# Order of the recurrent matrix products in one LSTM step: two products of the low part of h moved one place forward

## The reference, cut to what matters

```python
def step(carry, xs):
    h, c = carry
    i_t = sigmoid(xi_t + h @ V_i)
    g_t = tanh(xg_t + h @ V_c)
    o_t = sigmoid(xo_t + h @ V_o)
    c_new = h * c + i_t * g_t
    h_new = o_t * tanh(c_new)
    return (h_new, c_new), h_new
```

## Time and profile before

| what | us |
|---|---|
| median of three runs | 19581.66 |
| lowest, highest | 19550.09, 19586.31 |
| span of the profiled execution | 17545.4 |
| recurrent products in it, from the first to the last | 9353.7 |

### The profile page before, as it was taken

The page is one execution under the profiler, slowest core; times in us unless marked ns, Lnnn a source line. Parts: engine busy times, 40 slices in busy tenths (PEclk is TensorE's granted clock), DMA queues, the critical chain, the costliest instruction groups (busy, mean ns, idle before and its releaser), DMA issues. The chain is left out here.

```text
span 17545.4 us, 683245 instructions
## 1 busy us (share of the span) xinstructions
PE 12730.7 (73%) x250869; PEld 10213.3 (58%) x250870; DVE 11697.3 (67%) x68713; ACT 5986.8 (34%) x41949; POOL 5631.1 (32%) x6174
## 2 busy tenths in 40 slices
PE   5247773399655656556888888888888888888887
PEld 3135552266444544445777777777777777777776
DVE  7368887322555454556777777777777777777777
ACT  0004442011100101003555555554555555555555
POOL 4778887666576575772000000000000000000000
PEclk6558886599877777775555555555555555555555
DMA  0102222111333333331000000000000000000000
GB/s 22 25 21 73 74 72 43 56 34 33 101 105 98 96 105 87 105 105 37 4 4 4 4 4 4 4 4 4 4 4 4 4 4 4 4 4 4 4 4 18
DMA packets 352412, 609.44 MB, mean 35 GB/s; under 512 B 157501, under 2 KB 232222, under 8 KB 348988
## 3 DMA queue, kind: packets, MB, share of 16 engines
q0 software_dynamic: 223104, 471.33, 10.4%
q1 hardware_dynamic: 126524, 100.27, 1.9%
HBM read 508.72 MB, written 62.45 MB: 33 GB/s over the span
## 5 line engine op out<-in xcount | busy, mean ns | idle before, releaser
L2402 PE MATMUL lr_ZI<-ls_h,ls_V 128*128 128x1 f16 x150000 | 5006.8, 166 | 1669.7 <-DVE ls_h L2451 1412.8
L2402 PEld LDWEIGHTS lr_ZI<-ls_h,ls_V 128*128 128x128 f16 x150000 | 4487.3, 104 | 2677.0 <-DVE ls_h L2451 2640.4
L2419 ACT ACTIVATE ls_tg<-lr_ZI 128x2 f32<-128x2 f32 x12500 | 2150.0, 172 | 4626.5 <-PE lr_ZI L2402 4534.6
L2446 DVE TENSOR_TENSOR_SCAN lr_c<-ls_tg,ls_one_hc 128x2 f32<-128x2 f32 x12500 | 2118.1, 170 | 1441.0 <-ACT ls_tg L2419 1317.8
L2358 POOL COPY ls_HT<-ls_h 128x250 f32 x50 | 19.8, 395 | 9358.3 <-DVE ls_h L2456 9358.3
L2402 PE MATMUL lr_ZO<-ls_h,ls_V 128*128 128x1 f16 x75000 | 2865.0, 165 | 0.0
L671 PE MATMUL prop_sum<-prop_G,prop_S 128*128 128x256 f32 x4992 | 1830.4, 546 | 1369.9 <-DMA prop_G<-hop_table,prop_idx 1369.9
L657 POOL DMA_INDIRECT prop_G<-hop_table,prop_idx x2496 | 2368.3, 949 | 1057.3 <-issue 708.8
L2402 PEld LDWEIGHTS lr_ZO<-ls_h,ls_V 128*128 128x128 f16 x75000 | 2483.2, 104 | 0.0
L671 PEld LDWEIGHTS prop_sum<-prop_G,prop_S 128*128 128x128 f32 x4992 | 1403.9, 288 | 1796.3 <-issue 1486.1
L2451 DVE TENSOR_TENSOR ls_h<-ls_to 128x1 f16<-128x1 f32 x12500 | 2023.4, 162 | 479.1 <-ACT ls_to L2424 16.0
(11 more groups left out here) (455 smaller groups left out, 13965.7 us busy)
## 6 DMA issues: line engine op xcount, KB each, us to landing
prop_G<-hop_table,prop_idx POOLq DMA_INDIRECT x2496, 2.7
mow_W<-in_L_ffn_W SPq DMA_DIRECT2D x16, 1024.0 KB, 10.8
moe_out<-me_Ys SPq DMA_DIRECT2D x108, 128.0 KB, 1.7
all_X<-gat_table,gs_idx POOLq DMA_INDIRECT x832, 2.8
hop_table<-ht_T SPq DMA_DIRECT2D x50, 256.0 KB, 2.1
sd_records<-sc_rec,sc_place POOLq DMA_INDIRECT x784
ss_records<-me_recs,me_places POOLq DMA_INDIRECT x540
gat_table<-gt_hs SPq DMA_DIRECT2D x50, 128.0 KB, 1.8
```

Of the source, the lines that this page charges most:

```text
L2402: mm = nc.tensor.matmul(place(hf, bank, col, 1), (V2 if part == "21" else V1)[:, q, ROWS.index(row), :], hx[:, prev, q, 1:2], start=False, ...
L2419: nc.scalar.activation(tg[:, s % 2, m, :], place(hf, m, col, 2), ACT.Tanh, scale=back).then_inc(gates[m], 1)
L2446: nc.vector.tensor_tensor_scan(c[m][:, 0:2], tg[:, e, m, :], one_hc[:, m, :], 1.0, ALU.mult, ALU.add).then_inc(cell[m], 1)
```

## The change

It replaces `ORDER`. In both versions the list has the same 36 products.

```diff
-ORDER = (terms("i0 g0 i1 g1", "11 21", 0) + terms("i0 g0", "11 21", 1) + terms("i0 g0", "12", 0) + terms("i1", "11", 1)
-         + terms("i0 g0", "12", 1) + terms("i1", "21", 1) + terms("g1", "11 21", 1)
+ORDER = (terms("i0 g0 i1 g1", "11 21", 0) + terms("i0 g0", "11 21", 1) + terms("i0 g0", "12", 0)
+         + terms("i0 g0", "12", 1) + terms("i1", "11 21", 1) + terms("g1", "11 21", 1)
          + [t for q in range(KD) for t in terms("i1 g1", "12", q)]
          + [t for row in ("o0", "o1") for q in range(KD) for t in terms(row, "11 21 12", q)])
```

## The result

The changed kernel takes 19651.73 us (median of five runs, 19617.17 to 19665.10), the kernel before 19574.83 us (five runs, 19550.09 to 19586.31). The ratio is 1.0039 with a 95% interval of 1.0026 to 1.0052: slower, by 77 us between the medians.

What follows compares the result with a forecast made beforehand. Two circles of dependences, one per half, were taken to bound the 1480 ns step, half 0's ruling. A 9 ns stall over 6250 steps, 56 us, less 1, plus 2, gave +57 us on 19581.7: 19639 us, range 19572 to 19668.

Steps and rivals of the forecast that it cites:

- the sum: Recurrent layer: 9 ns over 6250 steps, 56 us, less 1 us, plus 2 us: +57 us, bounds +37 to +75.
- The price of a wait: PE weight loads: a load starts 53 ns after the DVE scan it waited for, also in mid-stream.
- the stall of 9 ns: Load 15, now waiting for h2 of half 1, starts at 380 instead of 371; bounds 6 to 12 ns.
- the circle of half 1: Load 15, bank 1, c, tanh, h1, h2 of half 1, load 15: claimed to rule at 1489 ns a step, not 1480.
- A sooner c is worth nothing: Half 0: bank 0 and c come 18 ns sooner, but the tanh goes by the sigmoid, through bank 2: 0 ns.
- 6 ns of slack: Tanh of c, half 0: starts 39 ns after its c, against 33 in half 1, so 6 ns of slack.
- The two small terms: -1 us for 96 steps waiting for ACT's clearing; about +2 us for some 90 steps already stopped for h2.
- Rival A: Load 15: its stall is absorbed, nothing gained or lost, 19582 us; chance 0.16.
- Rival B: L2424 of half 0: stall absorbed and tanh follows its c, 14 ns a step, 88 us faster, 19494 us; chance 0.04.
- Rival C: Load 15: the stall is a whole place, 27 ns a step, 167 us slower, 19749 us; chance 0.02.

Runs made afterwards that it cites:

- experiment 4: The kernel before, old order, with the wait for h2 of half 1 two products sooner, at product 14: 19812.1 us, 1.0123 of before.
- experiment 8: The kernel before with products 17 and 30 added into banks 1 and 3, so banks 0 and 2 both close one product sooner: 17478.2 us, 0.9955 of before.
- experiments 2: The kernel before with product 17 added into bank 1, so bank 0 closes with product 16, wait still at 16: 19553.1 us, 0.9989 of before.
- 3: The changed kernel with products of part 12, half 1, reading h2 of a step earlier, so nothing waits for the late h2: 19574.4 us, 0.9999 of before.
- experiments 5: The kernel before with products 17 and 18 exchanged, so bank 0 closes with product 18, waits as before: 17707.3 us, 1.0086 of before.
- 7: The kernel before with product 30 added into bank 3, so bank 2 closes with product 29, order and waits as before: 17553.7 us, 0.9999 of before.
- experiments 1: The kernel before, old order, with only the wait for h2 of half 1 moved to product 15: 19649.5 us, 1.0041 of before.

## Why the prediction was right, point by point

The forecast was 19639 us, the measured 19652; the sum had +57 us, measured are +64.5 and +77 us in the two comparisons, and 69.8 us in the stage. The +77 lies just above the sum's own bounds, +37 to +75. In the time less of this shows, because the forecast was set on a median of three runs, 19581.7, that is 7 us above the one of all five; that part of the agreement is luck.

*The price of a wait, 53 ns from the end of a DVE scan to the load, also in a stream.* Right: load 15 of the changed kernel stands still in every regular step, and on the same chip h2 of half 1 ends at 200 + 2590/20 = 330 and load 15 starts some 53 ns on, at 380 to 385 after the mark (12799.04 - 12798.657). The sums of the changed kernel there, marks from 12798.657 on, 1491.65 ns apart; the scan L2455, then PEld's first load:

```profile
sum 4.00, DVE 2.59; mean DVE 0.13
```

```profile
sum 2.70, PEld 2.01; mean PEld 0.10
```

The rule of the Trainium skill that was weighed ("TensorE: Matmul & The Clock Gate", "Step-by-step: what each phase is for"), that loads are pulled ahead of matmuls in flight, does not hide a load's own wait here: the stop at load 15 stands in the trace, and experiment 4 shows a further place of it paid nearly in full, 26.0 of 26.6 ns.

*The term that was mis-sized: the stall of 9 ns.* The marks are 1491.65 ns apart against 1480.65, 11 ns more. The sigmoid of half 0 starts at 1100 - 1790/20 = 1010.5 and PE's first load at 100 - 2010/20 = -0.5, while before on that chip has 1100 - 1980/20 = 1001 and 100 - 1950/20 = 2.5. Here the sums for L2422, after and before, and the one for PEld before:

```profile
sum 3.00, ACT 1.79; mean ACT 0.09
```

```profile
sum 3.00, ACT 1.98; mean ACT 0.10
```

```profile
sum 2.70, PEld 1.95; mean PEld 0.10
```

So bank 2 closes 12 to 13 ns later after PE's start instead of 9. Part of that is that h2 of half 1 itself falls back against PE's start by 2 to 3 ns (330 against 327.5, the latter 200 + 2600/20 less the 2.5). The sum took the relation of h2 to the first load from the kernel before, in which half 0 rules; once half 1 rules, that relation belongs to the other circle. The rest is 1 ns or so in the restart of the stream, which the rows of 10 ns do not resolve: averaged over all regular steps of the two traces, load 15 starts 12 ns later behind the first load (384 against 372) and load 18 13 ns later (465 against 452). The sum for L2455 of before on that chip:

```profile
sum 4.00, DVE 2.60; mean DVE 0.13
```

*The stall comes back each step, the circle of half 1.* Right: with the wait at 14, 15 and 16 its length is 1520, 1492 and 1467 ns. The first is experiment 4, where two first loads 20 steps apart start at 12814.46 and 12844.86; the last is experiment 8, where both other banks close sooner, with first loads at 12882.60 and 12911.93. I had put the middle one at 1489, 3 ns short. The same working gave 1462 for the last, 5 ns short, which the same term explains for the most part.

*A sooner c is worth nothing.* Right in the result: experiments 2 and 3, no gain. The changed kernel itself shows it too. Below are its sums for L2446, +0.950 to +1.030, and for L2424, +1.030 to +1.150, then the same two of before on that chip:

```profile
sum 1.60, DVE 1.24; mean DVE 0.06
...
sum 2.40, ACT 1.45; mean ACT 0.07
```

```profile
sum 1.60, DVE 1.55; mean DVE 0.08
...
sum 2.40, ACT 1.64; mean ACT 0.08
```

The new c of half 0 ends at 950 + 1240/20 = 1012, before at 1027.5; against PE's start that is 12 to 13 ns sooner and not 18, since the stall took more of the place. Its tanh starts at 1077.5, before at 1068, 67 ns behind the sigmoid in both. So the tanh goes with the sigmoid and lets c wait 65 ns where it was 40. Wrong is the 6 ns of slack in before: it is 1 to 3, as experiments 5 and 7 show. The forecast did not rest on its size, the expectations of 5, 7 and 8 did.

*The two small terms.* The 96 waits for ACT's clearing are in both kernels. The idle time of PE and PEld ahead of products that waited for h2 goes from 27.5 to 30.6 us, in the direction of the +2 us of the sum; no run tests either term alone.

*Rival A, absorbed:* falls by the interval of the ratio, and by experiments 1 and 4. *Rival B, faster:* falls by 2 and 3. *Rival C, a whole place:* falls too; 27 ns is what the second place costs, not the first.

No version came out that beats both kernels and computes the same. Experiment 8 says what it would need: banks 0 and 2 both closing a product sooner, with the wait for h2 not sooner than product 16. Bank 0 needs twelve products of its own, two of which read the late h2; with the wait at 16 it closes with 17. Bank 2 is behind all products of banks 0 and 1. So in this layout the order of before seems to stand already where the circles meet; that is argued from these counts, and other orders were not tried.

## What to carry to other kernels

In a serial recurrence, lay out each circle of dependences and ask by how much the longest leads the next, in ns and not in instructions. A product moved forward to close a bank sooner carries its wait with it, and the wait can lie on another circle: here a gain that only one of two level circles could feel was bought with 27 ns of room where 18 were free. Measure slack from end to end; starts of instructions that queue behind another mislead.

## What was not expected

- A tanh of one element on ACT lasts 171 ns in the record when released by its operand and 166 to 167 when it starts 67 ns behind another activation; the ends then differ by 1 to 3 ns where the starts differ by 6.
- The stages ahead of the recurrent layer, the same in all kernels here, differ by 2.0 ms between chips (8152.8 and 10184.7 us to the first recurrent product). With nothing stalled, the stage takes 9358.8 us in before on one, and 9363.6 and 9372.3 us in experiments 3 and 2 on the other. What makes either was not tried.
- Bank 0 one product later and bank 2 one product later cost the same 150 us, each alone; one product sooner each alone gave 0.1% and nothing.
